# A graph-and-expert layer on one core: the second norm's scale and shift moved to ScalarE's copies, VectorE's parts of a group cut finer

## What is computed

```python
xn = _layernorm(x, axis=-1)
x = x + gnn(xn, src, dst, ...) + mix(xn, ...)          # gnn ends in a norm, a 256x256 matmul, relu
# experts, on x1 = x:
xn = (x - mu) * rsqrt(var + EPS) * gamma + beta        # after an outer _layernorm(x)
logits = xn @ Wr + br                                  # 8 experts
top_vals, top_idx = top_k(logits, 2);  w = softmax(top_vals)
for e in range(8):
    h = gelu(xn @ W1[e] + b1[e]);  y_e = h @ W2[e] + b2[e]
    y = y + y_e * w_full[..., e, None]
return x + y
```

## Time and profile before

| | us |
|---|---|
| median of 3 runs | 4155.21 |
| runs | 4150.76 to 4159.93 |
| the profiled execution, its own time | 4158.91 |
| its span, first to last instruction | 4156.8 |
| stages one and two | 0 to about 3340 |
| last stage ahead of the first expert tile | 3340 to 3477.7 |
| expert tiles 0 to 34, and the wait for tile 35 | 3477.7 to 3722.8 |
| expert tiles 35 to 118 | 3722.8 to 4111.3 |
| last gathers, combines and stores | 4111.3 to 4156.8 |

### The profile page before, as it was taken

One profiled execution on the slowest core, in us unless ns is written; L12 is line 12 of the kernel. 1 busy time (PEld: TensorE's weight loads), 2 busy tenths in 40 slices (PEclk: granted clock), 3 DMA queues, 4 the chain that ended last, 5 costly groups with the idle time before them and its releaser, 6 DMA issues. The chain is left out here.

```text
span 4156.8 us, 84831 instructions
## 1 busy us (share of the span) xinstructions
PE 3271.1 (79%) x23505; PEld 2270.4 (55%) x23505; DVE 2657.3 (64%) x6011; ACT 1801.4 (43%) x4855; POOL 2805.5 (67%) x2698
## 2 busy tenths in 40 slices
PE   4888746777777777778999999999997747777995
PEld 1333324444444444445767777677775426666895
DVE  8888886666666666666666666666665463535222
ACT  2666532223223222224555555555553213444663
POOL 4466547888888888888888888888888713335233
PEclk7666658888888888988999999999998767989997
DMA  1222113343334334333333333333333333334354
GB/s 59 75 78 76 67 67 89 100 113 100 100 101 110 99 101 110 99 100 109 100 100 100 100 101 99 99 98 100 100 99 97 94 133 103 118 106 155 105 155 131
DMA packets 270014, 420.80 MB, mean 101 GB/s; under 512 B 75088, under 2 KB 198158, under 8 KB 269640
## 3 DMA queue, kind: packets, MB, share of 16 engines
q0 software_dynamic: 96112, 265.62, 23.0%
q1 hardware_dynamic: 150924, 132.95, 10.3%
q10 hardware_dynamic: 22860, 20.83, 1.8%
HBM read 334.91 MB, written 84.30 MB: 101 GB/s over the span
## 5 line engine op out<-in xcount | busy, mean ns | idle before, releaser
L800 POOL DMA_INDIRECT room<-table,room x1760 | 2084.0, 1184 | 472.7 <-issue 454.7
L1909 PE MATMUL bank<-room 128*128 128x260 f32 x3520 | 1015.6, 439 | 362.6 <-DVE room L1442 331.5
L1909 PEld LDWEIGHTS bank<-room 128*128 128x128 f32 x3520 | 729.3, 217 | 533.9 <-issue 419.8
L1433 DVE TENSOR_TENSOR room<-bank,room 128x16 f32<-128x16 f32 x440 | 76.7, 174 | 837.6 <-DMA room<-table,room 514.8
L1442 DVE TENSOR_TENSOR room<-room 128x1024 f32<-128x1024 f32 x440 | 535.7, 1218 | 12.3 <-ACT room L1024 11.4
L1024 ACT ACTIVATE room<-room 128x16 f32<-128x16 f32 x440 | 94.7, 215 | 902.6 <-DVE room L1436 880.9
L1462 DVE TENSOR_TENSOR room<-room 128x1024 f32<-128x1024 f32 x392 | 476.9, 1217 | 0.0
L1015 ACT ACTIVATE away<-bank,minus_p 128x512 bf16<-128x512 f32 x440 | 300.2, 682 | 378.1 <-PE bank L1885 377.8
L1831 PE MATMUL bank<-room 128*128 128x264 f32 (+1 forms) x588 | 312.6, 673 | 64.6 <-issue 34.4
L1018 ACT ACTIVATE spare<-away,ones 128x512 bf16<-128x512 bf16 x440 | 317.6, 722 | 54.1
L1421 DVE TENSOR_TENSOR room<-iota_f,row_step 128x512 f32<-128x512 f32 x440 | 303.4, 690 | 0.4 <-DVE room L1411 0.2
(11 more groups left out here) (308 smaller groups left out, 5083.3 us busy)
## 6 DMA issues: line engine op xcount, KB each, us to landing
room<-table,room POOLq DMA_INDIRECT x1760
kv_dram<-room SPq DMA_DIRECT2D x49, 324.0 KB, 2.2
room<-kv_dram SPq DMA_DIRECT2D x196, 81.0 KB
y_dram<-planes SPq DMA_DIRECT2D x119, 128.0 KB, 1.8
room<-xs_dram ACTq DMA_DIRECT2D x110, 128.0 KB, 2.2
q_dram<-room SPq DMA_DIRECT2D x49, 192.0 KB, 1.8
room<-q_dram SPq DMA_DIRECT2D x196, 48.0 KB
table<-room SPq DMA_DIRECT2D x49, 130.0 KB, 2.1
```

Of the source, the lines that this page charges most:

```text
L800: pool.indirect_dma_start(G[:, k.slot, u, :], None, table, bass.IndirectOffsetOnAxis(ap=ixbuf[:, k.slot, u:u + 1].bitcast(I32), axis=0)).t ...
L1909: ins = pe.matmul(pbank[1 + h][:, 0:TW], OH[:, s, u, :], Gw[:, h, u, :], start=(u == 0), stop=(u == U - 1))
```

## The change

- gamma and beta are no longer folded into the router and the experts: the work of L1182, L2126, L1783 and their small companions goes. Instead ACT applies them as it copies transposed tokens, where a feature lies on a partition: the second-phase copies (part 5, L1122) become Identity with a scale and a bias read per partition, and `copy_tile` becomes two such activations of 128x128 in the place of one copy of 128x256.
- DVE's part 0 is cut in 0 and 0b (variance), its part 3 in 3 (take the products), 3b (L1622, L1624) and 3c (variance). Each has its own tile in `SKEW`; all later parts move back, a group now spans 13 tiles for 11.
- Group 4 begins at tile 17 for 18, group 5 at 10 for 0 and group 6 at 22 for 10 of batch 1's tiles. The list stands 13 tiles after the last begin, not 11.
- Ahead of the loop, DVE's part 6 of group 0 now stands before part 4 of group 1.

```diff
-    SKEW = {"dve": {0: 0, 1: 1, 3: 4, 4: 6, 6: 9, 7: 10, 8: 11}, "act": {2: 3, 5: 8, 7: 10}, "pe": {2: 3, 3: 4, 5: 8, 6: 9, 8: 10},
-            "pool": {0: 0, 2: 4, 3: 5, 8: 11}, "sp": {1: 1, 2: 4, 3: 7, 5: 8}}
-    BEGIN = {0: (0, 9, 18), 1: (0, 10)}
+    SKEW = {"dve": {0: 0, "0b": 1, 1: 2, 3: 5, "3b": 6, "3c": 7, 4: 8, 6: 12, 7: 13, 8: 13}, "act": {2: 4, 5: 10, 7: 13},
+            "pe": {2: 4, 3: 5, 5: 10, 6: 12, 8: 13}, "pool": {0: 1, 2: 5, 3: 7, 8: 13}, "sp": {1: 2, 2: 5, 3: 7, 5: 7}}
+    BEGIN = {0: (0, 9, 17), 1: (10, 22)}
...
-                due_parts[name][BOFF[b] + begins[-1] + 11].append((b + 1, "list"))
+                due_parts[name][BOFF[b] + begins[-1] + 13].append((b + 1, "list"))
...
-                    o.mark(act.activation(xT[:, c, 2 * j * P:(2 * j + w) * P], pbank[j % 2][:, c * 2 * P:(c * 2 + w) * P], ACT.Copy))
+                    if ph:
+                        o.mark(act.activation(out, src, ACT.Identity, scale=gm[:, c:c + 1], bias=bt[:, c:c + 1]))
+                    else:
+                        o.mark(act.activation(out, src, ACT.Copy))
...
-            act.activation(xT_t[:, n % 2, :, :].rearrange("p c n -> p (c n)"), pbank[3][:, 0:2 * P], ACT.Copy).then_inc(xt_copied4, 1)
+            for c in range(2):
+                ins = act.activation(xT_t[:, n % 2, c, :], pbank[3][:, c * P:(c + 1) * P], ACT.Identity, scale=gm[:, c:c + 1], bias=bt[:, c:c + 1])
+            ins.then_inc(xt_copied4, 1)
...
-        act.wait_ge(s_b1, 1)
-        for e in range(XE):
-            for kc in range(2):
-                part = w1[:, e, kc * HID:(kc + 1) * HID]
-                o.mark(act.activation(part, part, ACT.Copy, scale=gm[:, kc:kc + 1]))
-        o.settle()
-        act.wait_ge(b1_done, 1)
+        act.wait_ge(w1_in, 16 * XE)
...
+            if part == "0b":
                 variance(g, xg, 1.0, LN_EPS)
...
+            if part == "3b":
                 dve.wait_ge(ff_copied, (g + 1) * GT)
...
-
+            if part == "3c":
                 variance(g, gb, 1.0 + LN_EPS, LN_EPS * LN_EPS)
...
-        for g, part in ((0, 0), (0, 1), (1, 0), (1, 1), (0, 3), (0, 4), (1, 3), (1, 4), (0, 6), (0, 8), (0, 7), (1, 6), (1, 8)):
+        for g, part in ((0, 0), (0, "0b"), (0, 1), (1, 0), (1, "0b"), (1, 1), (0, 3), (0, "3b"), (0, "3c"), (0, 4),
+                        (1, 3), (1, "3b"), (1, "3c"), (0, 6), (1, 4), (0, 8), (0, 7), (1, 6), (1, 8)):
```

More of the change, by code:

```diff
@@ L405, in _build @@
     s_wb = sem("s_wb")
-    s_b1 = sem("s_b1")
-    b1_done = sem("b1_done")
     w1_taken = sem("w1_taken")
@@ L467, in _build @@
         for b, begins in BEGIN.items():
-            todo = [(BOFF[b] + at + skew[part], part < 6, g, part) for g, at in zip(range(*BATCHES[b + 1]), begins) for part in skew]
-            for n, _, g, part in sorted(todo):
+            todo = [(BOFF[b] + at + skew[part], part not in (6, 7, 8), g, i, part) for g, at in zip(range(*BATCHES[b + 1]), begins) for i, part in enumerate(skew)]
+            for n, _, g, _, part in sorted(todo):
                 due_parts[name][n].append((g, part))
             if name in ("dve", "pool"):
-                due_parts[name][BOFF[b] + begins[-1] + 11].append((b + 1, "list"))
+                due_parts[name][BOFF[b] + begins[-1] + 13].append((b + 1, "list"))
     ENDS = TILES + GT * (BATCHES[-1][1] - BATCHES[-1][0]) + 2
@@ L1121, in copy_transposed @@
                     w = min(2, GT - 2 * j)
-                    o.mark(act.activation(xT[:, c, 2 * j * P:(2 * j + w) * P], pbank[j % 2][:, c * 2 * P:(c * 2 + w) * P], ACT.Copy))
+                    out, src = xT[:, c, 2 * j * P:(2 * j + w) * P], pbank[j % 2][:, c * 2 * P:(c * 2 + w) * P]
+                    if ph:
+                        o.mark(act.activation(out, src, ACT.Identity, scale=gm[:, c:c + 1], bias=bt[:, c:c + 1]))
+                    else:
+                        o.mark(act.activation(out, src, ACT.Copy))
                 o.settle()
@@ L1761, in _ @@
             o.mark(dve.tensor_scalar(ffw[:, c, :], ffw[:, c, :], gn_g[:, c:c + 1], None, ALU.mult))
-            o.mark(dve.tensor_scalar(wr[:, c, :], wr[:, c, :], gm[:, c:c + 1], None, ALU.mult))
-        o.mark(dve.tensor_tensor(br[0:XE, :], br[0:XE, :], pbank[2][0:XE, C:C + 1], ALU.add))
         o.settle()
@@ L1780, in _ @@
         segments(1)
-        dve.wait_ge(s_b1, 1)
-        b1 = w1[:, :, 2 * HID:W1W]
-        dve.tensor_tensor(b1, b1, pbank[5][:, 0:4 * XE].rearrange("p (e c) -> p e c", e=XE), ALU.add).then_inc(b1_done, 1)
         dve.wait_ge(s_wb, 16)
@@ L2114, in _ @@
         for c in range(2):
-            pe.matmul(pbank[2][:, 0:C], gn_bb[:, c, :], ffw[:, c, :], start=(c == 0), stop=(c == 1))
-        for c in range(2):
-            ins = pe.matmul(pbank[2][0:XE, C:C + 1], wr[:, c, :], bt[:, c:c + 1], start=(c == 0), stop=(c == 1))
+            ins = pe.matmul(pbank[2][:, 0:C], gn_bb[:, c, :], ffw[:, c, :], start=(c == 0), stop=(c == 1))
         ins.then_inc(s_fold, 1)
@@ L2121, in _ @@
             prepare(g, part)
-        pe.wait_ge(w1_in, 16 * XE)
-        for e in range(XE):
-            for c in range(4):
-                for kc in range(2):
-                    ins = pe.matmul(pbank[5][:, 4 * e + c:4 * e + c + 1], w1[:, e, kc * HID + c * P:kc * HID + (c + 1) * P], bt[:, kc:kc + 1],
-                                    start=(kc == 0), stop=(kc == 1))
-        ins.then_inc(s_b1, 1)
         pe.wait_ge(s_w4e, 16 * XE)
-        pe.wait_ge(b1_done, 1)
         turn_tile(0)
```

## The result

The changed kernel is slower by 0.15%: 4161.34 us (median of 17 runs, 4155.70 to 4169.19) against 4155.32 us for the kernel before on the same chip (17 runs, 4150.14 to 4166.05), ratio 1.0015, 95% interval 1.0008 to 1.0022. The forecast was 4147 us with a range of 4131 to 4160; the time lies above both. In two more sets of runs the same kernel stood at 1.0017 (1.0003 to 1.003) and 1.0018 (1.001 to 1.0027). So the difference is small, but it has the same sign and size three times.

The account below looks back on a forecast made before the run. From tile 35 on, PE's own work was taken as the floor, with waits mostly from POOL's queue above it. 5.6 - 8.9 + 0.4 - 5.2 = -8.1 us from 4155.2 gave 4147, range 4131 to 4160.

Parts of the forecast that it names:

- The price of one affine copy: ACT's 128x256 activation with scale and bias per partition: 600 ns against 424, so 0.18 us more, bounds 0.10 and 0.20.
- Part 5's term: Eight affine copies in a row on ACT, PE waiting for the last: 1.4 us more, part 5 from 6.67 to 8.1.
- Stretch one, +5.6: Ahead of the first expert tile: later logits and DVE's part 6 before group 1's norm cost 5.6 us, bounds 3.0 to 6.2.
- Stretch two, slots at 73.8, 137.4 and 198.5: Tiles 0 to 34: groups 2, 3, 4 get slots these us after the first transposes; 8.9 us gained, 0.4 lost to copies.
- Both new waits: PE waits about 6.4 us for `routed` before group 4's part 3, and 14.4 us for group 6's norm behind group 5's scatters.
- Stretch three, -5.2: Tiles 35 to 118, to the last pair of second matmuls: 379.8 us in place of 385.0, 5.2 less.
- The removed fold gains nothing: Ahead of the first tile, folding gamma and beta lies beside POOL's chain of scatters and clears, so removing it gains nothing.
- The hidden affine: Rival: part 5's copies cost their lower bound and DVE's slots don't wait for the Exp; up to 10 us, 4137, chance 0.22.
- the 1/std that doesn't bind: Rival: POOL reaches group 6's 1/std behind the scatters early enough, saving 14.4 + 1.9 us; 4131, chance 0.12.
- The clock rival: Rival: whole rounds at 1.2 GHz after six waits of 5 to 14 us, two more at the start; +18 us, 4165, chance 0.15.
- Table loads: Rival: Identity outside Gelu's table set, two loads per tile on ACT; about 220 us more, 4370, chance 0.03.
- What to look for: Signs listed: first tile about 3483, slots at 74, 137, 198, unchanged DVE L843 waits, both new PE waits, ACT idle 0.7.

Follow-up runs that it names:

- set D: Runs on one chip, kernel before 4155 us: changed kernel 1.0018, 1/std ahead of another group's scatters 0.9984, needless transposes 0.9984, scatters spread 0.9877.
- the kernel with the clock kept up: Changed kernel plus 20 needless transposes a group in TensorE's part 5 waits for ScalarE's copies: 4149.80 us, 0.9984 of the kernel before; changed kernel beside it 4164.02.
- the kernel of the order alone: Changed kernel's new step order and finer DVE parts, with both folds kept and plain copies: 4144.80 us, 0.9968 of the kernel before; on a slower chip 0.9915.
- the best version: Changed kernel with router folded again, group 1's norm and the 1/std moved earlier, scatters spread two a tile: 4105.18 and 4106.20 us; experts folded too, 4108.12.
- a kernel of 4139: Changed kernel with gamma and beta folded into the router again, part 5's copies plain, experts' copies still affine: 4138.73 us, 0.9962 of the kernel before.
- set E: Runs on one chip, kernel before 4160 us: new order with both folds 0.9968; scatters-spread kernel with and without the experts' fold, both 0.9869.
- set C: Runs on one chip, kernel before 4613 us: needless transposes 0.9859, scatters spread 0.9776, both folds with norm and 1/std moved 0.9940.
- sets A and C: Runs where the kernel before took 4630 and 4613 us; the former: new order only 0.9915, affine only 0.9973, norm earlier 0.9885, 1/std earlier 0.9912.

## Where the prediction was right and where it failed

- **The price of one affine copy: right.** 559 ns for 381 ns (128x256): 0.18 us, as taken.
- **Part 5's term, "8 x 0.18 = 1.4 us (bounds 0.8 to 1.6)": the step that failed.** It is 3.2 us in group 2 (9.83 for 6.67): 1.46 for the copies, as forecast, and 1.70 for the logits at the lower clock, a term that the sum put at nothing. In group 3 the logits alone cost 2.87 more. I summed the copies and held TensorE's own work fixed, though its waits there grew from 0.41 and 0.91 us to 0.77, 0.49 and 1.64. The test by needless transposes prices the omission at 14.2 us in set D, where the changed kernel stood 9.3 us above the kernel before and so 17.4 us above the forecast of -8.1. The other 3.2 us are the errors of the stretches below, which partly cancel. In the first set of runs the miss was 14.3 us; that this is so near 14.2 is chance.
- **Stretch one, +5.6: the mechanism right, the size too small.** The step in DVE's order and the later logits are there, and GpSimd's first scatter comes 10.8 us later in the profile (3436.30 - 3340.7 against 3425.96 - 3341.2), 6.5 in the kernel with the clock kept up (5.6 forecast), 2.5 in the one without affine copies (bound 3.0). With the clock kept up 4.3 us of the excess go (groups 0 and 1 had logits of 4.87 and 5.91 us); 0.9 stay open.
- **Stretch two, slots at 73.8, 137.4 and 198.5: right but for the clock.** GpSimd's first scatter, 0.4 us behind the slots, comes at 76.0, 142.4 and 204.9 us behind the first tile in the changed kernel, and at 74.1, 136.9 and 198.4 in the kernel with the clock kept up: 73.7, 136.5 and 198.0 for the slots. The 5.7 us by which stretch two fell short are the clock's: kept up, it gives 6.5.
- **Both new waits: right** (6.2 and 13.2 us; 6.4 and 14.4 forecast, though 99.2 - 85.0, the terms of the second, make 14.2). The waits for VectorE's L1744 behind the scatters of groups 2 and 3 are 5.48 and 4.17 us in this profile (5.50 and 5.42 with the clock kept up), about the 6.6 forecast, for 12.6 each before.
- **Stretch three, -5.2: too good, by more than the clock.** Without the clock term it is still only 1.4 us shorter (388.8). Group 5's slots were counted 114.4 us behind the start of tile 35's round. In the kernel of the order alone, where 1.4 us less is due (113.0), they come at 3825.5 - 3707.8 = 117.7, 4.7 late. The rows show where most of it lies: tiles 45 to 57 have waits of 0.69, 0.68, 2.22 and 1.07 us, 4.7 in all, that I had put at about 1.2. VectorE has the combines of the batch before in its rounds there; that these cause the waits was not tested, and the last 1.2 us are not placed. The timeline of three of them on TensorE in that kernel:

```profile
3760.98 1.09 PE L2041 MATMUL bank<-ident,room 128*128 128x128 f32 x8 [0.69 <-DVEq L1616]
...
3793.61 2.00 PE L2112 MATMUL bank<-room 128*128 x8 [2.22 <-DVE planes L1746]
3796.68 1.06 PE L2041 MATMUL bank<-ident,agg 128*128 128x128 f32 x8 [1.07 <-issue]
```

- **The removed fold gains nothing: right** where its cover holds. The order alone with the fold has a first stretch of 139.0 us, TensorE idle 18.84 us behind the fold, and the best version has 137.0 with the experts' fold and 136.9 without.
- **The rivals.** The hidden affine and the 1/std that doesn't bind fell. The clock rival gave 4165 us, near the measured 4161, but by luck and not by its own mechanism: it put the low clock into the rounds behind the long waits of 5 to 14 us. What the forecast lacked sat in part 5, behind three waits of 0.5 to 1.6 us. Table loads fell: ScalarE has 11 in the last stage, as many as before, and Identity stands between Gelus without one.
- **What to look for** was named well for both new waits and, but for the clock, for the slots. VectorE's waits for the mix bias of groups 3 and 4 were to be about as long as before (12.54 us) and were 8.74 and 7.49. Part 5, which the working puts at 8.1, was not on that list; it was the row by which the miss could be read at once.

## What to carry to other kernels

An operation made dearer on an engine that TensorE waits for can be paid twice, as it was in most groups here: once as the longer wait, once in the matmuls behind it, at the granted clock that has fallen. So price it by the row of the matmuls behind the wait, and by the granted clock over them, not by the copies alone. Ask of each half of such a change which engine's idle time hides it: here 0.43 us a tile on ScalarE cost nothing, while 1.4 us a group in TensorE's way added 21 us to a kernel of 4139, what the clock took with it included. Where a queue holds a long burst of one kind (fourteen scatters, 18 us), spreading it over the tiles can be worth as much as taking a step out from behind it: 12.7 us of one stretch here, against 13.5 for the 1/std.

## What the runs showed of the hardware

- With waits of 0.77, 0.49 and 1.64 us between and behind a group's transposes the granted clock was 0.65 and 0.52 over the matmuls behind them in groups 2 and 3 of the changed kernel, while waits of 0.41 and 0.91 us in the same place left group 2's at 1.00 in the kernel before.
- It isn't the same each time. With the same waits, group 6's logits ran at 3.17 us in the changed kernel (1.63 us of wait ahead of them) in all three of its profiles, and group 1's and 2's in one of them. Over all profiles the logits were slower than 3.17 us in 39 of 49 groups with affine copies, in none of 14 with affine copies and the waits filled, and in 2 of 70 with plain copies. Of these two, one had waits of 0.41 and 1.07 us (the order alone, set E), the other waits of 4.38, 1.72 and 0.66 us (scatters spread, set C; 5.89 us).
- Twenty 128x128 transposes of nothing, 2.7 us of TensorE's time a group in its waits, kept the clock at 1.00 over the logits (group 2, set D), and the kernel was 14.2 us shorter.
- In sets A and C, TensorE's waits for nothing that the profile names come to 23 to 61 us in the last stage (11 to 40 of them, up to 8.6 us long); in all other profiles they come to 4 to 8 us (1 to 4 of them). Work that is covered in the other sets (the fold) ended a stretch there, and one gain of 13.5 us showed as 4.8. A ratio from there doesn't carry over: two variants that differ from the changed kernel in one step stood at 0.9885 and 0.9912 in A, and one of them at 0.9984 in D. What those waits are was not tested.
